# Routing weights of a mixture-of-experts layer spread over the partitions by DMA through DRAM

## The reference, cut to what matters

```
x = x + L0_conv(groupnorm(x))            # graph-like mixing, once, in the set-up
t = tokens(x)                            # 4096 tokens of 64 features
t = t + L1_attn(layernorm(t))            # selective scan over 256 tokens per image
t = t + L1_ffn(layernorm(t))             # router + 8 experts, the part that is changed
```

```
logits  = xt @ Wr + br                   # [tokens, 8]
probs   = softmax(logits)
top_p, top_idx = top_k(probs, 2)
weights = top_p / top_p.sum(-1)          # two non-zero weights per token
h = gelu(einsum('end,edh->enh', xe, W1) + b1)   # every expert on every token
y = einsum('enh,ehd->end', h, W2) + b2
out = (weights[:, :, None] * sel).sum(axis=1)
```

## Time and profile before

| what | us |
|---|---|
| median of three runs (lowest, highest) | 408.23 (407.21, 408.71) |
| the profiled execution, its own time | 409.93 |
| its span | 408.20 |
| step 5, from one t1s (L792) to the next | 255.38 to 295.15 |
| busy in the whole span: PE, DVE, ACT, POOL | 338.1, 337.5, 281.3, 265.9 |
| copies of `wbs` by ACT (L626), 32 of them | 19.2 |
| matmuls that spread the weights (L1164) | 16.1 |

### The profile page before, as it was taken

One profiled execution on the slowest core, in us unless ns is written; L12 is line 12 of the kernel. 1 busy time (PEld: TensorE's weight loads), 2 busy tenths in 40 slices (PEclk: granted clock), 3 DMA queues, 4 the chain that ended last, 5 costly groups with the idle time before them and its releaser, 6 DMA issues. The chain is left out here.

```text
span 408.2 us, 5461 instructions
## 1 busy us (share of the span) xinstructions
PE 338.1 (83%) x1642; PEld 181.1 (44%) x1642; DVE 337.5 (83%) x462; ACT 281.3 (69%) x458; POOL 265.9 (65%) x270
## 2 busy tenths in 40 slices
PE   0597897677999789888988997899789878998694
PEld 0484445333454445344534552455245424544352
DVE  2774458998999999999999999999999988995411
ACT  1002667498978987998799879987887757761462
POOL 9706112986569947994898589758975984593122
PEclk9996999589899999999999999999988986999899
DMA  8761079899899588658975697579667950000000
GB/s 195 204 134 26 2 189 223 216 227 224 203 222 227 138 206 205 163 123 197 219 177 137 153 239 169 146 174 220 151 162 176 230 124 0 2 0 13 2 0 13
DMA packets 21236, 59.52 MB, mean 146 GB/s; under 512 B 4924, under 2 KB 13272, under 8 KB 15320
## 3 DMA queue, kind: packets, MB, share of 16 engines
q1 hardware_dynamic: 20040, 58.34, 61.7%
q10 hardware_dynamic: 1168, 0.84, 0.8%
HBM read 53.93 MB, written 5.24 MB: 145 GB/s over the span
## 5 line engine op out<-in xcount | busy, mean ns | idle before, releaser
L345 POOL TENSOR_TENSOR hs<-hs,Cs 128x1024 f32<-128x1024 f32 x63 | 149.2, 2372 | 44.9 <-DVE hs L767 44.3
L767 DVE TENSOR_TENSOR_SCAN hs<-av,P 128x1024 f32<-128x1024 f32 x64 | 146.3, 2287 | 4.7 <-ACT av L576 1.3
L633 ACT ACTIVATE hb<-P,b1c 128x512 f32<-128x512 f32 x128 | 81.6, 684 | 18.8 <-PE P L1177 16.3
L760 DVE SCALAR_TENSOR_TENSOR P<-P,bbcol,ub 128x1024 f32<-128x1024 f32 x62 | 79.7, 1286 | 2.4 <-DMA ub<-u_scratch 1.2
L1190 PE MATMUL P<-hb,W2s 128*64 128x256 f32 x512 | 70.0, 397 | 0.0
L1176 PE MATMUL P<-X,W1H 128*128 128x512 f32 x128 | 60.4, 472 | 6.4 <-ACT hb L633 4.7
L576 ACT ACTIVATE av<-P,Aneg 128x510 f32<-128x510 f32 x68 | 44.1, 688 | 13.9 <-PE P L1130 10.0
L1177 PE MATMUL P<-X,W1L 128*128 128x512 f32 x128 | 52.3, 409 | 0.0
L357 POOL TENSOR_TENSOR accs<-accs,mes 128x256 f32<-128x256 f32 x56 | 40.9, 731 | 14.1 <-DVE mes L856 9.5
L1190 PEld LDWEIGHTS P<-hb,W2s 128*64 128x64 f32 x512 | 31.8, 138 | 31.4 <-issue 20.8
L856 DVE SCALAR_TENSOR_TENSOR mes<-P,cols,wbs 128x256 f32<-128x256 f32 x64 | 27.3, 468 | 17.4 <-PE P L1190 9.6
(11 more groups left out here) (190 smaller groups left out, 488.8 us busy)
## 6 DMA issues: line engine op xcount, KB each, us to landing
ub<-u_scratch SPq DMA_DIRECT2D x31, 1024.0 KB, 10.7
av<-dt_scratch SPq DMA_DIRECT2D x15, 1024.0 KB, 7.0
dt_scratch<-dts SPq DMA_DIRECT2D x7, 256.0 KB, 2.8
u_scratch<-rl SPq DMA_DIRECT2D x7, 256.0 KB, 2.8
av<-in_L_conv_Wr SPq DMA_DIRECT2D x2, 576.0 KB, 7.3
av<-in_L_conv_Wl SPq DMA_DIRECT2D x2, 576.0 KB, 8.1
res<-in_x SPq DMA_DIRECT2D x4, 256.0 KB, 4.8
hb<-in_L_ffn_W SPq DMA_DIRECT2D x2, 512.0 KB, 6.3
```

The source lines that it names most:

```text
L345: gp.tensor_tensor(hs[:, at, :, :], hs[:, at, :, :], rep(Cs[:, p, :], 1, 2), ALU.mult).then_inc(S["cm"], 1)
L633: a_.activation(hb[:, r % 4, :], P[:, (XA, XB)[r % 2], :], ACT.Gelu, bias=b1c[:, r:r + 1]).then_inc(S["gl"], 1)
L760: v.scalar_tensor_tensor(out=ring, in0=rep(P[:, BB, :], 1, 2), scalar=bbcol[:, 0:1], in1=ub[:, 2 * n:2 * n + 2, :], op0=ALU.add, op1=ALU.m ...
L767: v.tensor_tensor_scan(hs[:, (SLOTS * g + n) % RING].rearrange("p a t -> p (a t)"), av[:, 2 * n:2 * n + 2, :].rearrange("p a t -> p (a t)" ...
```

## The change

Four things change.

1. The weights are spread by DMA. ACT copies `wT` (now 16x256, fp32), waits until the copy is written, and issues a DMA of it to a DRAM scratch `w_scratch`. SP waits for that DMA, and issues six DMAs that read it back into `wbs`, 64 partitions each: experts 0 and 1, 2 and 3, 4 to 7, for each image. `pe_wb`, `act_wb`, `selW` and the split into two parts are gone.
2. SP issues these six DMAs between chunk 0 and chunk 1 of `sp_spread`, so that chunk 1 comes behind them and behind their wait for `wt_out`.
3. The router's bias is the first matmul of the logits' accumulation on PE (identity times `brs`), in place of DVE's addition.
4. ACT writes the exponential to PSUM (`chances`), DVE's marks go to PSUM (`ranked`), the first three router operations stand between the two halves of `X2`, and the normalisation of the group after next (`dve_xn`) stands inside the router chain in place of behind it.

In the set-up, POOL no longer builds `selWf` (one memset and two affine_selects on 32x1024) and DVE no longer copies it.

```diff
+    w_dram = nc.dram_tensor("w_scratch", (2, 2 * EXP, HW), fp32, kind="Internal").ap()
...
+        chances = P[:, XC, 64:64 + 4 * EXP].rearrange("p (c e) -> p c e", e=EXP)
...
             for c in range(CHUNKS):
+                if c == 1 and g >= 2:
+                    sp_weights(sp_, g - 2)
                 since(sp_, "scan", SLOTS * (g - 1) + 2 * c + 2)
...
+        def sp_weights(sp_, g):
+
+            sp_.wait_ge(S["wt_out"], 16 * (g + 1))
+            if g == 0:
+                sp_.wait_ge(S["ffn_l"], 1)
+            since(sp_, "me", EXP * g)
+            for r, (lo, hi) in enumerate(((0, 2), (2, 4), (4, 8))):
+                for h in range(2):
+                    sp_.dma_start(wbs[64 * h:64 * h + 64, lo:hi, :],
+                                  rep(w_dram[g % 2][EXP * h + lo:EXP * h + hi, :], 0, 64)).then_inc(S[f"wb{r}"], 16)
...
-            gp.memset(selWf[:, :, :, :], 0.0).then_inc(S["k_zero"], 1)
...
-            gp.tensor_copy(vv[:, :, :, 0, :].bitcast(f32r), w4).then_inc(S["vhi"], 1)
-            eng.wait_ge(S["vhi"], g + 1)
-            gp.tensor_tensor(vv[:, :, :, 1, :], w4, vv[:, :, :, 0, :], ALU.subtract).then_inc(S["vlo"], 1)
...
-            a_.activation(rt[:, 2], rt[:, 1], ACT.Exp).then_inc(S["ex"], 1)
+            a_.activation(chances, rt[:, 1], ACT.Exp).then_inc(S["ex"], 1)
...
+            a_.activation(wT[:, :], P[0:2 * EXP, XD, 0:HW], ACT.Copy).then_inc(S["wtc"], 1)
+            eng.wait_ge(S["wtc"], g + 1)
+            since(eng, "wb2", 32 * (g - 1))
+            eng.dma_start(w_dram[g % 2], wT[:, :]).then_inc(S["wt_out"], 16)
...
-            a_.activation(wbs[:, 2 * r:2 * r + 2, :].rearrange("p e f -> p (e f)"), P[:, YS, :], ACT.Copy).then_inc(S["wb"], 1)
...
-            v.tensor_tensor(biased, P[:, XC, 0:4 * EXP].rearrange("p (c e) -> p c e", e=EXP),
-                            rep(brs[:, :], 1, 4), ALU.add).then_inc(S["lgb"], 1)
...
-            v.scalar_tensor_tensor(out=rt[:, 3], in0=rt[:, 2], scalar=1.0, in1=rank[:, :, :], op0=ALU.is_ge, op1=ALU.mult).then_inc(S["s1"], 1)
+            v.scalar_tensor_tensor(out=ranked, in0=chances, scalar=1.0, in1=rank[:, :, :], op0=ALU.is_ge, op1=ALU.mult).then_inc(S["s1"], 1)
...
+            if norm is not None:
+                dve_xn(eng, norm)
...
+                eng.wait_ge(S[f"wb{min(e // 2, 2)}"], 32 * (g + 1))
...
+            pe.matmul(P[:, XC, 0:4 * EXP], ident[:, :], rep(brs[:, :], 1, 4), start=True, stop=False).then_inc(S["lgb"], 1)
...
-                pe.matmul(P[:, YS, HW * (e % 2):HW * (e % 2) + HW], selW[:, e, :], wT[:, :],
-                          start=True, stop=True).then_inc(S["wb_mm"], 1)
```

More of the change, by code:

```diff
@@ L414, in _ @@
                              pattern=[[-BLK, NBLK]], channel_multiplier=1).then_inc(S["k_sel"], 1)
-            gp.affine_select(out=selWf[:, :, :, :], in_=selWf[:, :, :, :], compare_op=ALU.not_equal, fill=1.0, base=0,
-                             pattern=[[-1, EXP], [-2 * EXP, 2], [0, 64]], channel_multiplier=1).then_inc(S["k_sel"], 1)
-            eng.wait_ge(S["k_sel"], 3)
+            eng.wait_ge(S["k_sel"], 2)
             gp.affine_select(out=pv, in_=pv, compare_op=ALU.is_ge, fill=0.0, base=1,
@@ L810, in dve_xn2 @@
                 q = slice(64 * h, 64 * h + 64)
+                if h == 1 and between is None:
+                    dve_router1(eng, g)
                 v.tensor_tensor(X2[0:64, HW * h:HW * h + HW], P[q, XB, 0:HW], rqs[q, :], ALU.mult).then_inc(S["xh2"], 1)
         def dve_router1(eng, g):
-            biased = P[:, XC, 64:64 + 4 * EXP].rearrange("p (c e) -> p c e", e=EXP)
+            logits = P[:, XC, 0:4 * EXP].rearrange("p (c e) -> p c e", e=EXP)
             eng.wait_ge(S["lg"], 2 * (g + 1))
-            v.tensor_tensor(biased, P[:, XC, 0:4 * EXP].rearrange("p (c e) -> p c e", e=EXP),
-                            rep(brs[:, :], 1, 4), ALU.add).then_inc(S["lgb"], 1)
@@ L830, in dve_router2 @@
             eng.wait_ge(S["s1"], g + 1)
-            v.tensor_reduce(rv[:, 1], rt[:, 3], AX, ALU.max).then_inc(S["ms1"], 1)
+            v.tensor_reduce(rv[:, 1], ranked, AX, ALU.max).then_inc(S["ms1"], 1)
             eng.wait_ge(S["ms1"], g + 1)
-            v.tensor_tensor(rt[:, 4], rt[:, 3], bc(1), ALU.is_equal).then_inc(S["o1"], 1)
+            v.tensor_tensor(rt[:, 4], ranked, bc(1), ALU.is_equal).then_inc(S["o1"], 1)
             eng.wait_ge(S["o1"], g + 1)
-            v.scalar_tensor_tensor(out=rt[:, 5], in0=rt[:, 4], scalar=-2.0, in1=rt[:, 2], op0=ALU.mult, op1=ALU.add).then_inc(S["e2"], 1)
+            v.scalar_tensor_tensor(out=rt[:, 5], in0=rt[:, 4], scalar=-2.0, in1=chances, op0=ALU.mult, op1=ALU.add).then_inc(S["e2"], 1)
@@ L951, in _ @@
                                 rep(cT[:, ti, :], 2, n), ALU.add).then_inc(S["r_add"], 1)
[L953 removed]
+            eng.wait_ge(S["k_zero"], 7)
             for k in range(4):
                 v.tensor_copy(selS[:, k, BLK * k:BLK * k + BLK], mask8[:, :]).then_inc(S["k_selu"], 1)
[L956 to L957 removed]
+            eng.wait_ge(S["k_sel"], 4)
             eng.wait_ge(S["ld_wf"], 64)
@@ L1005, in body @@
                     dve_xn2(eng, prev)
-                    dve_router1(eng, prev)
-                    dve_router2(eng, prev)
-                if i > 0 and nxt2 is not None:
-                    dve_xn(eng, nxt2)
+                    dve_router2(eng, prev, nxt2)
                 dve_slot(eng, i, 2)
@@ L1367, in body @@
                     pe_f2(eng, prev, 1)
-                    for n in range(2, 6):
-                        pe_pair(eng, prev, n)
-                        pe_wb(eng, prev, n - 2)
-                    for n in range(6, 8):
+                    for n in range(2, 8):
                         pe_pair(eng, prev, n)
@@ L1407, in _ @@
             pe_f2(eng, G - 1, 1)
-            for n in range(2, 6):
-                pe_pair(eng, G - 1, n)
-                pe_wb(eng, G - 1, n - 2)
-            for n in range(6, 9):
+            for n in range(2, 9):
                 pe_pair(eng, G - 1, n)
```

66 lines of the change are left out of this document (20 added, 46 removed).

## The result

| | before | after |
|---|---|---|
| median of six runs each (lowest, highest), us | 408.97 (407.21, 410.58) | 413.51 (411.22, 413.92) |
| ratio, 95% interval | | 1.0102 (1.0067 to 1.0136) |
| profiled execution, its span | 409.93, 408.20 | 413.62, 411.90 |
| first t1s, last t1s, end of the span | 96.43, 373.42, 408.20 | 94.78, 379.01, 411.90 |
| so: set-up and step 0, steps 1 to 7, tail | 96.43, 276.99, 34.78 | 94.78, 284.23, 32.89 |

The changed kernel is 1.0% slower; 404.5 was forecast.

A forecast was written before the change was run, and what follows sets the result against it. DVE's list was taken to set a step's length. The terms -4.7 + 1.0 + 3.1 - 2.3 - 0.8 = -3.7 gave 406.2 us for the profiled execution and 404.5 for the median, range 400 to 410.

The forecast's parts named there:

- Weights wait, steps 2 to 6: DVE's first expert waits for the weights through DRAM, which just fit: 0.2 us per step, +1.0 in all.
- Step 1: The first weights queue behind chunk 0 on busy DMA engines, so DVE waits: +3.1 us (0 to 5).
- They are used a step later, so they cost nothing: Chunks 1 to 3 come 4.8 us later by the weights' 1 MB, at a cost of 0.
- Router: L829's successor on DVE no longer stalls beside POOL: 0.7 us less per step, -4.7 in all (0 to -7.0).
- Tail: No L816, no wait of PE for POOL (0.6 together), gelu pairs closer (1.7): -2.3 us (-1.0 to -3.0).
- Set-up: Without selWf POOL finishes before DVE's L875, so the group norm comes earlier: -0.8 us (0 to -1.2).
- (c): Rival: PE idles longer at step ends and its clock drops, 2.5 us each in five steps: 417 us; chance 0.13.
- (b): Rival: no measurable change, as L829's stall stays or moves, or weights come 0.7 us later per step: around 408; chance 0.17.

The follow-up runs named there:

- Weights between the two loads: The changed kernel with SP issuing the six weight loads between the av and the ub load of chunk 0: 411.79 us, ratio 1.0075.

## Why the prediction was wrong, step by step

- **Weights wait, steps 2 to 6: forecast +1.0, measured 8.5 of waits.** This is the step that failed. "I take 2.7 with the issue" for ACT's DMA was taken as if nothing large stood ahead of it. The write took 3.3 to 6.1. The prediction had the load's landing, 272.7, and asked of it only whether the second leg would be queued behind it; the first leg was too, in spite of its own queue. Had the write been put at 272.7, the first weights would have been due at 272.7 + 0.6 + 2.8 = 276.1, 0.5 us late. The other 0.9 of the 1.44 in step 5: the write landed 0.2 behind the load, the second leg took 3.9 (278.44 to 282.36) in place of 3.4, and DVE stood at its expert 0.2 earlier. In step 6 the write landed 1.4 behind the load, and DVE waited 2.78. Weights between the two loads (1.4 us of landing in steps 2 to 6, no wait there) shows that the first leg is the cause. The trace of the kernel before had it already. The 3.2 us of the earlier trace rows are of a write on ACT's queue, issued at 72.28, with the end of a 1 MB load of SP's queue ahead of it. In its first 1.1 us it moved nothing, and all the packets were SP's (the DMA view of the kernel before, 72.28 to 73.4):

```profile
q1 hardware_dynamic: 32, 0.26, 109.9%
```

  Two slips of the sum are small beside it: 269.1 + 2.7 is 271.8 and not 271.9, and both legs at 3.2 give 0.5 us of wait per step and not the 1.5 of the range.
- **Step 1: +3.1 forecast, 6.4 measured.** Only in part the same failure. That the weights stand behind chunk 0 was foreseen. But chunk 0 landed at 119.2, 24.4 us behind the step's t1s, where the kernel before gave 22.1 (118.5 - 96.43): that is 2.4 of the 3.3 us. The first weights were asked for at 116.7 and not "by 115", and DVE had them 2.0 behind the load in place of 1.2. Why the load was later is not shown; it was issued 0.8 later behind t1s and took 12.7 in place of 11.1.
- **"They are used a step later, so they cost nothing"** was false for `av` of chunk 1, but as long as DVE waits for the weights, the second chain is hidden (POOL does not wait for `av` in the changed kernel). It decides what mending the first is worth. Each measured against the kernel before of its group, the chain of kernels reads: no DMAs for weights -9.7; their traffic added -7.3; SP's wait ahead of chunk 1 added -2.0; DVE's wait added, the changed kernel, +4.5. That is about 2.4 (not clear of noise), 5.3 and 6.5 us.
- **Router: -4.7 forecast.** Right in kind. In step 5 it gave 1.0 in place of 0.7 (39.77 to 38.76), because with the marks the next slot stands 0.92 closer, where 0.8 were taken, and the exponential begins 0.13 earlier after t1s (6.62 in place of 6.75), where the prediction took it 0.1 later; and 8.0 in all, with the clock of step 7 and the tail. In the changed kernel it was worth 2.8 only, since it is not in the loop that sets the step. I summed it as if DVE stayed the bound.
- **Tail: -2.3 forecast, -1.9 measured**, with PE at 0.50 for 6.7 us in it. PE alone was late next, as said. The pairs gave 1.75 and the way to the exponential 0.22; the 0.34 at POOL's wait did not come.
- **Set-up: -0.8 forecast, 1.65 earlier in the two profiles.** L875's successor, L874, takes 0.17 us, as said. The first t1s lies between 95.1 and 96.4 in four kernels with the old set-up and between 94.6 and 97.0 in eight with the new one, so a gain can't be told from the scatter of the first loads.
- **Rivals.** (c) named slower, through the clock: not so in steps 2, 4 and 5, with 1.00. It was 0.96 in step 3, whose 40.02 us are the shortest of steps 2 to 5, and 0.89 in step 1 behind the wait (before: 1.00 and 0.96). That the kernel is slower, as (c) said, is no point for its mechanism. (b) named the right quantity, "the weights come 0.7 us later than I take", and stopped at no change. A rival in which the write waits for the load was missing.

The Trainium skill speaks to this leg in two places (DMA: Bandwidth & Descriptors, section Queues, rings and completion order). Its arbitration rule says that a DMA engine takes turns between its queues, and drains a whole packet, typically some 9 to 17 descriptors, from one before it switches. Its packets are thus bundles. What the profile counts as a packet of the large load is a single move of 8 KB (0.39 MB in 48), so 1 MB is 128 of them, 8 for each of 16 engines, and can be a single bundle on each, an estimate from that page's figure. By that rule the write waits for the rest of the load, and the trace agrees, with no packet of it in 2.0 us. How large a bundle is, no run here shows. The same section says that a semaphore's increment lands only behind all earlier writes of that engine, across queues. That too would make the landing late, but here the packets are already late, not only the semaphore, and no run tells the two apart.

## What to carry to other kernels

A small DMA can cost what was issued ahead of it, whichever queue it is in (here 1.4 us with nothing ahead, up to 8.3 with loads of 1 MB ahead): ask of each leg of a chain through DRAM, the write too, what was issued shortly before. A wait put into a list of issues is paid by every load behind it; look for who needs those loads first, memsets and restarts too. And a gain on an engine holds only while that engine is the bound: parts of a change that put another loop in charge swallow the others, so time them apart.

## What the runs showed of the hardware

- The landing of one and the same 16 KB write on ACT's queue: 1.4 us with nothing in flight, 2.7 to 8.3 with one or two loads of 1 MB in flight, 7.2 to 8.1 with a 1 MB load and six smaller ones issued just ahead.
- An operation of DVE on 128x8 elements with both inputs in SBUF stood for 3.20 us beside a row of POOL's operations, where it takes 0.17 in the changed kernel. The router's first mark took 973 ns in the median with both inputs in SBUF, and 199 to 200 ns in all of its occurrences with one of the two in PSUM.
